# A two-layer graph network with a mixture of experts: four groups per degree product, row statistics on two engines, and a later turn of the tokens in layer 2

## The reference

```python
def _gcn_conv(x, src, dst, ew, W, b, n_nodes):
    xW = x @ W
    deg = jax.ops.segment_sum(ew, dst, num_segments=n_nodes) + 1.0
    dinv = jnp.where(deg > 0, jax.lax.rsqrt(deg), 0.0)
    norm = dinv[src] * ew * dinv[dst]
    agg = jax.ops.segment_sum(norm[:, None] * xW[src], dst, num_segments=n_nodes)
    agg = agg + (dinv * dinv)[:, None] * xW
    return agg + b
...
    x = x + _L0_gnn_ref(_layernorm(x, axis=-1), edge_index, edge_weight, W1, b1, W2, b2)  # two relu(_gcn_conv)
    x = x + _L0_ffn_ref(_layernorm(x, axis=-1)[None], router_w, w1, b1, w2, b2)[0]        # 8 experts, top 2, gelu
```

## Time and profile before

| what | value |
|---|---|
| median of 3 runs | 4470.57 us (4467.15 to 4471.99) |
| the profiled execution's own time | 4468.36 us |
| its span | 4466.6 us |
| PE busy | 3671.5 us (82%) |
| DVE busy | 2554.7 us (57%) |
| ACT busy | 773.6 us (17%) |
| POOL busy | 3036.1 us (68%) |
| mean granted clock of PE, in parts of full | 0.91 |
| DRAM traffic | 445.14 MB read, 38.67 MB written |

### The profile page before, as it was taken

How to read it: one execution, slowest core, us unless ns; L and a number is a source line. 1 busy time by engine, 2 the same in 40 slices (tenths; PEclk the granted TensorE clock), 3 DMA queues, 4 the chain that set the end, 5 groups by cost and what they waited for, 6 DMA issues and landing times.

```text
span 4466.6 us, 79360 instructions
## 1 busy us (share of the span) xinstructions
PE 3671.5 (82%) x27380; PEld 3437.6 (77%) x27381; DVE 2554.7 (57%) x8924; ACT 773.6 (17%) x2385; POOL 3036.1 (68%) x3196
## 2 busy tenths in 40 slices
PE   6856666666666666666599999999999999999999
PEld 5646666666666556656589999999999999999999
DVE  7623333232232323333268888888888888888887
ACT  1300000000000000000012222222222222222222
POOL 2167777777777777777677666666666666666663
PEclk9978888888888888888789999999999999999999
DMA  6343333333333333333433333333333333333332
GB/s 147 109 143 112 112 112 111 112 111 112 111 112 112 111 112 111 112 112 111 109 113 112 106 106 106 105 105 105 106 106 106 106 106 106 107 106 107 106 106 59
DMA packets 243150, 489.19 MB, mean 110 GB/s; under 512 B 60006, under 2 KB 141225, under 8 KB 242748
## 3 DMA queue, kind: packets, MB, share of 16 engines
q0 software_dynamic: 150528, 411.24, 32.6%
q1 hardware_dynamic: 84424, 66.74, 4.9%
q10 hardware_dynamic: 7796, 6.06, 0.5%
HBM read 445.14 MB, written 38.67 MB: 108 GB/s over the span
## 4 chain that ended last, share of the span: by engine, by line
PE 45%; POOL 32%; issue 12%; DVE 7%; DMA 3%; ACT 0%; DVEq 0%; SPq 0%; ACTq 0%; POOLq 0%
POOL msg L485 31%; PE part L840 16%; PE psH L825 12%; PE psY L834 12%; DVE sel L1137 2%; DMA msg<-ytab,srcT 2%; DVE work L1226 1%; DVE nt L1219 1%; PE psT L807 1%; PE psH L840 1%; DVE work L1261 1%; DMA ytab<-msg 1%; PE psT L815 1%; PE psY L710 1%; DVE rs L1221 1%
## 5 line engine op out<-in xcount | busy, mean ns | idle before, releaser
L485 POOL DMA_INDIRECT msg<-ytab,srcT x3136 | 2988.1, 953 | 1270.8 <-issue 894.8
L840 PE MATMUL part<-sel,msg 128*128 128x96 f32 x8384 | 1120.2, 294 | 244.0 <-DMA msg<-ytab,srcT 244.0
L840 PEld LDWEIGHTS part<-sel,msg 128*128 128x128 f32 x8384 | 1094.1, 211 | 271.2 <-DMA msg<-ytab,srcT 226.4
L825 PEld LDWEIGHTS psH<-work,wbuf 128*128 128x128 f32 x6272 | 809.6, 192 | 35.4
L1137 DVE TENSOR_SCALAR sel<-iota,relT,ewT 128x96 f32<-128x96 f32 x3136 | 835.6, 341 | 2.2 <-ACT accbuf L557 1.3
L834 PE MATMUL psY<-wbuf,work 128*128 128x256 f32 x3136 | 824.8, 386 | 0.0
L825 PE MATMUL psH<-work,wbuf 128*128 128x128 f32 x6272 | 812.4, 275 | 0.0
L606 ACT ACTIVATE work<-psH,b_s 128x128 f32<-128x128 f32 x1568 | 491.1, 364 | 1582.5 <-PE psH L825 1582.5
L1145 DVE TENSOR_TENSOR accbuf<-accbuf,part 128x192 f32 x524 | 184.8, 353 | 716.5 <-PE part L840 716.4
L834 PEld LDWEIGHTS psY<-wbuf,work 128*128 128x128 f32 x3136 | 535.9, 191 | 40.6 <-ACT work L606 0.3
L840 PE MATMUL psH<-sel,msg 128*128 128x96 f32 x2080 | 356.0, 352 | 208.0 <-DMA msg<-ytab,srcT 208.0
(11 more groups left out here) (190 smaller groups left out, 2241.0 us busy)
## 6 DMA issues: line engine op xcount, KB each, us to landing
msg<-ytab,srcT POOLq DMA_INDIRECT x3136
ytab<-xS SPq DMA_DIRECT2D x99, 128.0 KB, 1.9
ytab<-msg SPq DMA_DIRECT2D x98, 128.0 KB, 1.8
xS<-in_x SPq DMA_DIRECT2D x98, 128.0 KB
out<-res SPq DMA_DIRECT2D x98, 128.0 KB
accbuf<-in_x SPq DMA_DIRECT2D x97, 128.0 KB, 3.1
wbuf<-in_L_ffn_w ACTq DMA_DIRECT2D x2, 2048.0 KB, 14.9
wbuf<-in_dst SPq DMA_DIRECT2D x1, 588.0 KB
```

What stands on the lines that cost most here:

```text
L485: pool.indirect_dma_start(msg[:, r * GT + j, :], None, ytab[l], bass.IndirectOffsetOnAxis(ap=srcT[:, g * GT + j:g * GT + j + 1].bitcast(U3 ...
L825: mm = pe.matmul(psH[e % 2][:, m * P:(m + 1) * P], w1_s[:, e, k, m * P:(m + 1) * P], tokS[s.u][:, k, :], start=(k == 0), stop=(k == KD - 1))
L840: m = pe.matmul(slot[:, h * W:(h + 1) * W], msg[:, tile0 + j, h * P:(h + 1) * P], sel[:, sel0 + j, :], start=(j == 0), stop=(j == GT - 1))
```

## The change

**In the degree loop.** One product now takes four groups at a time (QG = 4): `wlo` of four groups side by side (64 columns) as weights, `whi` of the same four (24 columns) moving, so 8 products in a step in place of 32. Of the 4 x 4 blocks of a result only the diagonal is used; the copies behind the turn pick it. `digits` writes the low digits in an order that puts the four groups side by side. The turns 2 to 15 move into PE's steps 0 to 13. ACT's list begins with its copies of the turns, without the waits for all edge loads, and the loads of the layer weights are issued behind the `gtab` stores.

**Statistics.** DVE keeps `bn_stats` for the 49 even blocks, four steps late. ACT takes the 49 odd blocks in two passes each, a `Copy` and a `Square`, with sums along the row (`accum_out`). These stand in ACT's list behind the 16 copies of turns and behind the `gtab` stores and their wait.

**Behind the loop.** All four `window_columns` and `node_columns` now stand behind it. `tables()` is split: its first 15 operations and the rest (`slots()`) both stand behind the loop as well. The square root of the norm's scale and its reciprocal come before the degrees are known.

**The table stage.** PE turns two blocks into one PSUM bank, and ACT copies two blocks with one instruction (49 in place of 98). The `dtab` store and load stand behind these copies, ahead of the loads of the expert weights.

**Layer 2.** In PE's list `turn_tok` stands behind group 2 and no longer ahead of it.

```diff
 # PE, degree loop
+        turn(0)
+        turn(1)
         for t in range(NS):
...
-            for r in range(SG):
-                at_col = (t % SB * SG + r) * HI
+            for u in range(SG // QG):
+                at_col = (t % SB * (SG // QG) + u) * QG * HI
                 for k in range(GT):
-                    m = pe.matmul(wbanks[t // SB][0:LO, at_col:at_col + HI], wlo[:, h, r * GT + k, :], whi[:, h, r * GT + k, :],
+                    lo4, hi4 = u * QG * GT + k * QG, slice(u * QG * GT + k, (u + 1) * QG * GT, GT)
+                    m = pe.matmul(wbanks[t // SB][0:QG * LO, at_col:at_col + QG * HI],
+                                  wlo[:, h, lo4:lo4 + QG, :].rearrange("p r n -> p (r n)"), whi[:, h, hi4, :],
                                   start=(k == 0), stop=(k == GT - 1))
             m.then_inc(s_wmm, 1)
+            if t + 2 < NTR:
+                turn(t + 2)
...
-            for c in range(GC - 1):
-                if t == (c + 2) * SB + 1:
-                    window_columns(c)
-                if t == (c + 2) * SB + 3:
-                    node_columns(c)
-        window_columns(GC - 1)
+        window_columns(0)
+        for c in range(1, GC):
+            window_columns(c)
+            node_columns(c - 1)
         node_columns(GC - 1).then_inc(s_cols, 1)
 # ACT
-        act.wait_ge(s_dst, 48)
-        act.wait_ge(s_ew, 48)
-        act.wait_ge(s_src, 48)
+        act.preload_act_table(ACT.Square)
...
+        def means(i):
+            b = 2 * i + 1
+            act.wait_ge(s_x[b // XS], XS * 16)
+            wait(act, s_mean, i)
+            act.activation(unread[0], xblock(b), ACT.Copy, scale=-1.0 / D,
+                           accum_out=minus_mean[:, i:i + 1]).then_inc(s_mean, 1)
+
+        def squares(i):
+            act.wait_ge(s_mean, i + 1)
+            wait(act, s_square, i)
+            act.activation(unread[1], xblock(2 * i + 1), ACT.Square, bias=minus_mean[:, i:i + 1],
+                           accum_out=square_sum[:, i:i + 1]).then_inc(s_square, 1)
...
+            while done < t:
+                means(done)
+                if done:
+                    squares(done - 1)
+                done += 1
...
             act.wait_ge(s_wmm, t)
-            act.activation(win[:, :, g:g + groups], wbanks[n][0:LO, 0:groups * HI].rearrange("l (g h) -> l h g", h=HI),
+            act.activation(win[:, :, at_s:at_s + steps], wbanks[n][0:QG * LO, 0:steps * QG * HI].rearrange("l (s c) -> l c s", c=QG * HI),
                            ACT.Copy).then_inc(s_win, 1)
...
+        for b in range(0, NB, 2):
+            act.wait_ge(s_y1T, b + 2)
+            act.activation(accT[:, :, PAD + b * P:PAD + (b + 2) * P].rearrange("p k (b n) -> p k b n", b=2),
+                           y1banks[b // 2 % XS][:, :].rearrange("p (b k n) -> p k b n", b=2, k=KD), ACT.Copy).then_inc(s_y1C, 1)
 
         act.wait_ge(s_dinv, 1)
...
-        for b in range(NB):
-            act.wait_ge(s_y1T, b + 1)
-            act.activation(xblock(b), y1banks[b % XS][:, 0:D].rearrange("p (k n) -> p k n", k=KD), ACT.Copy).then_inc(s_y1C, 1)
         act.dma_start(w1_s, ew1.rearrange("e (k p) n -> p e k n", p=P)).then_inc(s_experts, 16)
 # DVE, degree loop
+        LAG = 4
...
-            for b in (2 * t, 2 * t + 1):
-                statistics(b)
+            if t >= LAG:
+                statistics(t - LAG)
...
+        v.wait_ge(s_square, NH)
+        v.tensor_scalar(mean2[:, 1:NB:2], minus_mean, -2.0, None, ALU.mult)
+        link(v.tensor_scalar(lnscale[:, 1:NB:2], square_sum, 1.0 / D, EPS, ALU.mult, ALU.add))
+        v.sem_inc(s_var, 1)
+        tables()
         v.wait_ge(s_cols, 1)
         v.tensor_copy(cols[:, OH:OC], cbanks[1][0:W, 0:OC - OH]).then_inc(s_colsD, 1)
+        v.wait_ge(s_std, 1)
+        link(v.reciprocal(lnscale, lnscale))
+        slots()
 # PE, layer 2
-            if s:
-                turn_tok(s)
             if g:
                 group(1, R * i + 2)
+            if s:
+                turn_tok(s)
```

More of the change, by code:

```diff
@@ L44 @@
 SG = 8
+QG = 4
 ST = SG * GT
@@ L102, in build @@
     at[0] = 3 * GW
-    stats = behind(NB * 6).rearrange("p (b t) -> p b t", t=6)
     winT = behind(GC * W, GQ)
@@ L148, in build @@
     loT, hiT, dstT = msgw[:, 0:NT], msgw[:, NT:2 * NT], msgw[:, 2 * NT:3 * NT]
+    NH = NB // 2
+    stats = msgw[:, 3 * NT:3 * NT + NH * 6].rearrange("p (b t) -> p b t", t=6)
+    minus_mean, square_sum = (msgw[:, 3 * NT + (6 + n) * NH:3 * NT + (7 + n) * NH] for n in range(2))
     lo_i, hi_i = loT.bitcast(I32), hiT.bitcast(I32)
@@ L180, in build @@
     yS = xS
+    unread = [t.rearrange("p (k n) -> p k n", k=KD) for t in (xS[1][:, :], b2_s[-1][:, :])]
     h1, h1T = tok, tokS[0]
@@ L531, in _ @@
+        done = 0
         for n in range(len(wbanks)):
             t = min((n + 1) * SB, NS)
-            g, groups = n * SB * SG, (t - n * SB) * SG
+            while done < t:
[3 more added lines that the diff above has]
+                done += 1
+            if n == 3:
+                act.wait_ge(s_rwt, 1)
+                act.activation(rwT[:, :, :].rearrange("p k e -> p (k e)"), psT[:, 0:KD * NEXP], ACT.Copy).then_inc(s_rwt, 1)
+                act.activation(b1_s[:, :, :].rearrange("p e k -> p (e k)"), psT[:, 32:32 + NEXP * KD], ACT.Copy).then_inc(s_rwt, 1)
+            at_s, steps = n * SB * (SG // QG), (t - n * SB) * (SG // QG)
@@ L539, in _ @@
+        for c in range(GC):
+            act.wait_ge(s_winT, c + 1)
+            act.activation(winT[:, c * W:(c + 1) * W].rearrange("s (h l) -> s h l", h=HI),
+                           psH[c % 2][0:GQ, 0:HI * QG * LO].rearrange("s (h l) -> s h l", h=HI)[:, :, c * LO:(c + 1) * LO],
+                           ACT.Copy).then_inc(s_winC, 1)
         act.wait_ge(s_cols, 1)
@@ L667, in _, with turn @@
         pe.wait_ge(s_const, 3)
-        for n, (a, c) in enumerate(turns):
+        def turn(n):
+            a, c = turns[n]
             tile = (rel_g, ew_g, src_f, dst_f)[a]
@@ L934, in _ @@
                 hidden(last, 6)
+            if g:
+                group(1, R * i + 2)
             if s:
                 turn_tok(s)
-            if g:
-                group(1, R * i + 2)
             if last:
@@ L1033, in tables, with slots @@
             link(v.tensor_scalar(tgeneral[:, :], plain, -1.0, 1.0, ALU.mult, ALU.add))
+            v.sem_inc(s_tables, 1)
+        def slots():
             link(v.tensor_scalar(taken, taken, plain, None, ALU.mult))
@@ L1052, in tables, with statistics @@
             v.sem_inc(s_tables, 1)
-        def statistics(b):
-            if b % XS == 0:
-                v.wait_ge(s_x[b // XS], XS * 16)
-            v.bn_stats(stats[:, b, :], xblock(b)).then_inc(s_stats, 1)
-        chunks = 0
+        def statistics(i):
+            v.wait_ge(s_x[2 * i // XS], XS * 16)
+            v.bn_stats(stats[:, i, :], xblock(2 * i)).then_inc(s_stats, 1)
+        LAG = 4
+        chunks = have = 0
         for t in range(NS):
             h = t % 2
-            if (t + 1) * ST > chunks * GQ * GT:
+            if (t + 1) * ST > have:
                 v.wait_ge(s_edgeC, 2 * chunks + 1)
-                digits(relT, LO.bit_length() - 1, slice(chunks * GQ * GT, (chunks + 1) * GQ * GT))
                 chunks += 1
+                upto = chunks * GQ * GT // (QG * GT) * (QG * GT)
+                digits(relT, LO.bit_length() - 1, slice(have, upto), True)
+                have = upto
             wait(v, s_wmm, t - 1)
@@ L1089, in _ @@
-        link(v.tensor_tensor(sq, even[:, :, 2], odd[:, :, 2], ALU.add))
-        link(v.scalar_tensor_tensor(sq, sq, 1.0 / D, dif, ALU.mult, ALU.add))
-        link(v.tensor_scalar(lnscale, sq, EPS, None, ALU.add))
+            if t >= LAG:
+                statistics(t - LAG)
+        for i in range(NH - LAG, NH):
+            statistics(i)
+        v.wait_ge(s_stats, NH)
+        even, odd = stats[:, :, 0:3], stats[:, :, 3:6]
+        link(v.tensor_tensor(mean2[:, 0:NB:2], even[:, :, 1], odd[:, :, 1], ALU.add))
```

95 lines of the change are left out of this document (47 added, 48 removed).

## The result

The changed kernel takes 4392.41 us in the median of 4 runs (4391.92 to 4393.83), the kernel before 4470.55 us (4 runs, 4467.15 to 4471.99) beside it. The ratio is 0.9828, interval 0.9812 to 0.9844: 78 us less. That is 13 us above the forecast of 4379 and inside its range of 4361 to 4412, though 2 us beyond the case *as summed* (4370 to 4390).

The account below looks back on a forecast made before the run. The degree loop was read as engines waiting in turn, the table stage as DMA, layer 1 as POOL's gathers, layer 2 as PE's. Savings of 55 + 30 + 1.4 + 5 = 91.4 us gave 4379 us, range 4361 to 4412.

Parts of the forecast that it names:

- as summed: Whole kernel: the main case, all terms come as added up, 4370 to 4390 us; chance 0.55.
- Layer 2: Turn of the tokens behind group 2: PE's wait of 0.57 us goes in 96 of 98 iterations, -55 us.
- Start of the loop: Degree loop: without the waits for edge loads, PE's first product comes at about 19.5 us instead of 34.16.
- The product: Degree loop: a 64-column product instruction costs 0.067 us, 1.07 us a step (bounds 0.43 and 1.92).
- my 112: Degree loop's end: ACT's statistics, begun at about 65 us, end the loop at 112, 5 us after DVE.
- No engine is full: Old degree loop, 119 us: PE busy 98.7, DVE 93.8, the engines take turns in waiting.
- Statistics on ACT: Degree loop: a pair of ACT passes over a block costs 0.9 us (0.66 to 1.25), 49 pairs 44 us.
- Behind the loop: From loop end through node products: these end at 127.6 us, not 157.8, -30 us; then -1.4 to the first block.
- Table stage: Stage of 63.8 us: the moved `dtab` store and expert loads save 5 us (bounds 0 and -12.8).
- Fewer, wider ACT copies change nothing: Table stage: copying two blocks per ACT instruction gains nothing, as ACT was busy only 11.4 of 15 us.
- the set-up gives less: Before layer 1: pairs of 1.25 us, a dearer product or no table-stage gain, 4390 to 4410 us; chance 0.23.
- The two of layer 2: PE's wait only moves, 4434 us, chance 0.06; or new waits make it slower than before, chance 0.03.

Follow-up runs that it names:

- e1_turn_only: The kernel before with only the turn of the tokens moved behind group 2; 4413.33 us, ratio 0.9877.
- e2_turn_back: The changed kernel with the turn of the tokens put back ahead of group 2; 4444.44 us, ratio 0.9946.
- e9_more_stats: The changed kernel with one more `bn_stats` a step on DVE, result unread; 5005.44 us where the kernel before takes 5001.49.
- e8_half_products: The changed kernel with every second degree product left out, so half of the edges are missing; 4372.6 us, ratio 0.9789.
- e13_24x64: The changed kernel with the loop product's operands turned round (24 weight columns, 64 moving) and 20 products ahead of the first turn; 4377.45 us, ratio 0.9804.
- e3_dtab_ahead: The changed kernel with the `dtab` store and load back ahead of ACT's copies; 4395.41 us, ratio 0.9836.
- e4_quiet_tail: The changed kernel, but ACT waits until all block stores have landed before the `dtab` store and expert loads; 4383.77 us, ratio 0.9812.
- e12_wide_in_loop: The changed kernel with 60 wide products ahead of the first turn and four a step in the loop; 5130.15 us where the kernel before takes 5001.49.

## Why the prediction was right, and where it was off

**Layer 2: right.** 50.3 us against 55. A steady iteration takes 22.06 us (forecast 22.08), and no wait took the place of the removed one. In the medians the turn is worth 54.5 us (`e1_turn_only`) and 78.1 - 23.4 = 54.7 (`e2_turn_back`). In the profiled executions it is 50.3. From the first turn of the tokens to the last, 97 iterations took 2187.0 us before (22.55 on average) and 2134.8 after (22.01): 52.2 us, as of 91 or 92 iterations at 0.57. The same 97 took 2192.2 us in `e2_turn_back`, 57.4 more than in the changed kernel, so the missing part is the scatter of single executions. The first turn stands 1.6 us later behind the layer's start, since group 2 now goes first, and the end gives back 0.2.

**Start of the loop: right.** The first product was forecast at 19.5 and came at 19.48. The turn in a step was right by luck: it was put at eight instructions of 0.11 us, 0.9; it is four of 0.21, 0.84.

**The product: the term that was mis-sized.** The 64-column product was put at 0.067 us, 1.07 us a step; it costs 0.107, 1.71 us a step, near the upper bound of 0.12. The step that failed is the interpolation between a row of the loop (16 columns, 0.027) and a row of layer 2 (128 columns, 0.12), which belong to different levels of the clock. At the loop's level both ends are 1.67 ns a column: 16 columns 0.027, 64 columns 0.107, 128 columns 0.213. So 16 instructions of 0.107 cost as much as the 64 of 0.027 did, 1.71 against 1.75 us a step. The products of four groups saved nothing on PE. (The Trainium skill, TensorE: Matmul & The Clock Gate, section LDWEIGHTS (loading the stationary operand), puts a load at P / 1.2 ns for P columns, by which I estimate 0.053 us for 64; the measured 0.107 of an fp32 product instruction is twice that, and from 64 to 128 columns it grows in proportion to P, as the page says.)

From this one term the rest of the loop follows. Steps with a turn took 2.65 us in place of 2.0, so the turns ended at 58, not at 50. ACT, which stands behind them and the 13 us of the `gtab` stores, began its statistics at 72.7, not at 65. And the other 35 steps went by PE's 1.71, not by DVE's 1.33; the last copy came at 122.9 in place of 112. `e9_more_stats` shows that DVE wasn't the bound, `e8_half_products` and `e13_24x64` that with a cheaper product ACT ends the loop at 104 to 106, some 6 us before my 112. Their ACT started earlier, since the turns ended earlier.

The reading of the loop before was off too. "No engine is full" is an average: from 90 us on PE was busy 59.0 of 60 us, so fewer operations on DVE could not help there while the product's price stayed. What the loop gained, 15.7 us, is PE's idle time, which went from 20.4 to 4.9 us. No run separates its sources. At most 1.6 us of it is ACT's share of the statistics (`e9_more_stats`); `tables()` alone held PE idle for 6.3 of 9.1 us in the old loop, and the node products and the turns changed places with each other.

**Statistics on ACT: right.** The pair was taken as 0.9, the middle of wide bounds, and took 0.89: passes of 0.40 and 0.49, and a readout of 0.19 behind each, of which 0.09 pass before the next one starts. (The Trainium skill, ScalarE: Activation LUTs, section What ACT_TABLE_LOAD costs: its 0.399 for N = 256 agrees with the 0.40. The pair of 0.70 by it did not come about: it has no readout.)

**Behind the loop: right in its lengths.** From the last copy to the end of the node products it took 15.2 us (forecast 15.6); `tables()` and `slots()` cost nothing. But it began 11 us late, so the node products ended at 138.1, 19.7 us earlier than before and not 30. From there to the first block 10.7 us were left of 12.9, 2.2 less (forecast 1.4).

**Table stage: right in sign, small.** 2.4 us against 5. The order itself is worth the 5 us: set against `e3_dtab_ahead`, the changed kernel's stage is 5.0 shorter, DVE's wait of 4.76. But with the old order the new stage takes 66.4 us, 2.6 more than the 63.8 of before: the last store is issued 57.1 us behind the first scaled block in place of 55.7, and takes 8.29 to land in place of 7.06. "Fewer, wider ACT copies change nothing" is thus not shown; no run undoes them alone. The last stores were slow before as well, by the loads beside them; in the new order the words take over that part. `e4_quiet_tail` gives what the stage is worth without either, 9.5 us against the 63.8 of before. (The Trainium skill, DMA: Bandwidth & Descriptors, section Specifications, has transfers under 512 B read, modified and written back. By it the stage would have gained nothing; it gained 2.4. That the 256 words are slow agrees: 10.0 us from issue to landing beside a block store's 1.9.)

**The rivals.** Of "the set-up gives less", into whose 4390 to 4410 the result falls, one part came true, the dear product, without the dear pair. The two of layer 2 did not.

**What stays open.** On the chip with slower gathers, the changed kernel with the added statistics took 5005.44 us against 5001.49 of the kernel before: there the change gains nothing. The changed kernel as it is wasn't run there. POOL waits 478.6 us in all for what the profile calls `remote`, a wait that the changed kernel's trace doesn't have, and PE is busy only 371 of 400 us in the middle of layer 2, mostly with waits for other things than the tokens. That may be why the turn gains nothing; it isn't shown. Why the 22 us of the earlier first gather don't show either isn't known: the kernel before has no trace there.

## What to carry to other kernels

Take the price of a matmul from a row at the clock level at which it will run, and count the larger of its weight and moving columns: at 1.2 GHz, merging four products of 16 weight columns into one of 64 leaves the time the same. Whether it does at 2.4 GHz wasn't run. An engine that isn't full on average can be full in half of the stretch, so cut a stage until its slices look alike. A wait in front of an engine that is the bound is worth its whole length in every iteration, and an independent operation of the same engine is enough to fill it. Small scattered stores and big loads belong behind the landing of the stores that others wait for: `e4_quiet_tail`, the changed kernel with one such wait more, is the fastest complete kernel here with 4383.77 us, 84.1 us less than the 4467.86 of the kernel before on its chip.

## What the runs showed of the hardware

- A product instruction of this loop costs 1.67 ns for each column at 1.2 GHz, and it's the larger of the weight columns and moving columns that counts: 16x6 0.027, 16x24 0.040, 64x6 and 64x24 0.107, 24x64 0.10 to 0.11, 128x24 0.213 us. At 2.4 GHz 24x64 costs 0.062 and 16x24 0.027, somewhat more than half.
- PE can be busy almost without a gap and stay at 1.2 GHz: 98.6 of 103.5 us in the changed kernel's loop, and in `e12_wide_in_loop` even with four 128-column products in each step. With 64 moving columns in place of 24 (and 24 of weights in place of 64) it was at 2.4 GHz from the third step of the loop. No run here separates what decides it.
- The clock column reads 1.00 before its first change in a trace, whatever the level: the same weight load takes 0.333 us at 1.7 us and 0.192 at 8, both under 1.00.
- ACT's sum output is an instruction of its own, 0.19 us, and the next pass starts 0.09 us behind it.
- The last of 98 block stores of 128 KB lands after 1.84 us when nothing else is on the way, after 8.27 with a store of 256 single words beside it for the first 6.1 us and loads behind that, and after 8.29 with two loads of 2 MB.
- One chip moved 96 GB/s in layer 1's gathers where the changed kernel's moved 112, and the kernel before took 12% longer there.
